# Splitting V into two fp16 halves: from ScalarE and VectorE to GpSimd, through an fp32 copy of Wh in SBUF

## What is computed

```
h  = max(layernorm(x), 0)
Wh = h @ W                                   # 8 x 2048 x 256
f1 = Wh @ a[:256];  f2 = Wh @ a[256:]
e  = leaky_relu(f1[:, :, None] + f2[:, None, :], 0.2)
attention = softmax(where(adj > 0, e, -9e15), axis=1)   # over rows i, for each column j
out = x + elu(attention @ Wh)
```

## Time and profile before

| | |
|---|---|
| median of 3 runs | 992.19 us (990.35 to 992.49) |
| the profiled execution's own time | 987.88 us |
| its span, first to last instruction | 986.1 us |
| mean granted TensorE clock | 0.987 of full speed |
| busy: TensorE (PE) | 950.0 us, 96% |
| busy: VectorE (DVE) | 920.7 us, 93% |
| busy: ScalarE (ACT) | 879.3 us, 89% |
| busy: GpSimd (POOL) | 645.3 us, 65% |

### The profile page before, as it was taken

How to read it: one execution, slowest core, us unless ns; L and a number is a source line. 1 busy time by engine, 2 the same in 40 slices (tenths; PEclk the granted TensorE clock), 3 DMA queues, 4 the chain that set the end, 5 groups by cost and what they waited for, 6 DMA issues and landing times.

```text
span 986.1 us, 23861 instructions
## 1 busy us (share of the span) xinstructions
PE 950.0 (96%) x8993; PEld 840.0 (85%) x8993; DVE 920.7 (93%) x1271; ACT 879.3 (89%) x1237; POOL 645.3 (65%) x676
## 2 busy tenths in 40 slices
PE   8878999999999999999999999999999999999996
PEld 6666888889888898888888888888988989898896
DVE  8799989999899998999989998999999999999975
ACT  4788989999999999999999899999999999898985
POOL 6567665776766776876767776677676775555540
PEclk8899999999999999999999999999999999999898
DMA  9477667889879889799979988979987978979724
GB/s 233 83 107 108 97 108 122 147 162 156 149 136 176 146 155 167 119 180 149 161 147 144 173 148 151 154 141 172 156 163 123 172 133 138 170 113 158 143 65 140
DMA packets 199093, 142.13 MB, mean 144 GB/s; under 512 B 7361, under 2 KB 187841, under 8 KB 198978
## 3 DMA queue, kind: packets, MB, share of 16 engines
q0 software_dynamic: 140160, 81.80, 61.5%
q1 hardware_dynamic: 58818, 58.81, 20.8%
HBM read 176.16 MB, written 16.84 MB: 196 GB/s over the span
## 4 chain that ended last, share of the span: by engine, by line
POOL 32%; PE 30%; issue 25%; DVE 5%; DMA 4%; ACT 2%; POOLq 0%; SPq 0%; DVEq 0%; ACTq 0%
POOL direct L896 10%; POOL xn L910 6%; POOL raw L882 5%; POOL inv L893 4%; PE acc L511 4%; PE acc L504 4%; PE acc L506 4%; PE tp L439 3%; PE acc_st L486 3%; PE acc_st L487 3%; PE acc_st L488 3%; POOL y L916 3%; PE pre L417 3%; POOL rstd L904 2%; POOL small_total L890 2%
## 5 line engine op out<-in xcount | busy, mean ns | idle before, releaser
L773 DVE CUSTOM_DVE_ANT_0 prob<-tp,f_row 128x2048 f32<-128x2048 bf16 x128 | 292.0, 2282 | 21.5 <-DMA f_row<-f_scratch 14.9
L590 ACT ACTIVATE prob<-prob,f 128x2049 f32<-128x2049 f32 x128 | 257.6, 2013 | 5.4 <-DVE prob L773 5.4
L486 PE MATMUL acc_st<-v,stored 128*128 128x256 f16 x960 | 261.5, 272 | 0.8 <-ACT part L620 0.8
L488 PE MATMUL acc_st<-v,stored 128*128 128x256 f16 x960 | 261.7, 273 | 0.0
L487 PE MATMUL acc_st<-v,stored 128*128 128x256 f16 x960 | 261.6, 273 | 0.0
L598 ACT ACTIVATE prob<-prob,shift 128x2048 f32<-128x2048 f32 x128 | 256.5, 2004 | 4.0
L896 POOL TENSOR_TENSOR direct<-prob,inv 128x1024 f16<-128x1024 f32 x128 | 243.5, 1902 | 10.0
L504 PE MATMUL acc<-v,direct 128*128 128x256 f16 x1024 | 233.4, 275 | 5.4 <-ACT z_direct L626 3.5
L506 PE MATMUL acc<-v,direct 128*128 128x256 f16 x1024 | 233.3, 274 | 0.0
L890 POOL TENSOR_SCALAR small_total<-total 128x1 f32<-128x1 f32 x128 | 29.8, 233 | 272.8 <-ACT prob L598 271.4
L604 ACT ACTIVATE stored<-prob,inv 128x1024 f16<-128x1024 f32 x128 | 146.1, 1142 | 47.6 <-POOL inv L893 47.6
(11 more groups left out here) (94 smaller groups left out, 1383.9 us busy)
## 6 DMA issues: line engine op xcount, KB each, us to landing
raw<-in_adj POOLq DMA_DIRECT2D x64, 1024.0 KB, 11.2
y<-in_x SPq DMA_DIRECT2D x63, 256.0 KB, 3.1
out<-y SPq DMA_DIRECT2D x63, 256.0 KB, 2.2
y<-elu POOLq DMA_DIRECT2D x56, 256.0 KB, 5.0
x_in<-in_x SPq DMA_DIRECT2D x108, 128.0 KB, 3.3
f_row<-f_scratch SPq DMA_DIRECT2D x31, 256.0 KB, 6.5
stored<-in_x SPq DMA_DIRECT2D x4, 512.0 KB, 6.9
f_scratch<-f_t SPq DMA_DIRECT2D x124, 0.5 KB
```

The lines of the kernel that those rows point to most:

```text
L486: nc.tensor.matmul(bank[:, 0:FO], p_st[:, 0, rows], v_c[:, 0, :], start=(c == 0), stop=False)
L488: last = nc.tensor.matmul(bank[:, 0:FO], p_st[:, 1, rows], v_c[:, 0, :], start=False, stop=(c == G - 1))
L590: nc.scalar.activation(p_top, p_top, ACT.Prelu, bias=f2, alpha=ALPHA).then_inc(leaky, 1)
L773: nc.vector.tensor_tensor_reduce(out=prob[:, c % 2, 0:N], in0=tp_b, in1=f1_row[:, b % 2, :], scale=1.0, scalar=-3.0e38, op0=ALU.add, op1=A ...
```

## The change

The high and the low half of V are both made on GpSimd by a new function `split_v`. GpSimd gets them from `wh_sb`, a single fp32 buffer in SBUF into which ScalarE now copies Wh (`keep_wh`) where it made the high half before. VectorE's `split_v_low` stays for the first 17 chunks only. The next transpose into the bank waits for ScalarE's copy (`wh_kept`) in place of `v_ready`. The copy of chunk c waits until GpSimd has made both halves of chunk c - 1 (`v_ready`), and `split_v` is put between `split_high` and `normalise` in GpSimd's step. Each chunk's direct matmuls wait for `v_ready` of their own chunk, which is 17 steps old. A few small columns are packed together, and the ring of f2 columns shrinks from 20 to 18, to make room for `wh_sb`.

```diff
-    RF = 20
+    RF = 18
+        wh_sb = sb("wh_sb", [P, FO], F32)
-        minus_half = sb("minus_half", [P, 4], F32)
...
+        cols = sb("cols", [P, 16], F32)
+        minus_half, minus_one, small_total = cols[:, 0:1], cols[:, 1:2], cols[:, 2:3]
+        shift, total, inv = cols[:, 4:6], cols[:, 8:12], cols[:, 12:16]
# TensorE, transpose_x(c), c > LEAD
-                    wait(pe, v_ready, c)
+                    if c == LEAD + 1:
+                        pe.wait_ge(v_ready, LEAD)
+                    pe.wait_ge(wh_kept, c - LEAD)
# TensorE, direct_blocks(c)
-                    pe.wait_ge(v_ready, LEAD)
+                pe.wait_ge(v_ready, max(c + 1, LEAD))
# ScalarE
+            def keep_wh(c):
+                act.wait_ge(v_ready, c)
+                nc.scalar.copy(wh_sb[:], wh_bank(c)[:, 0:FO]).then_inc(wh_kept, 1)
...
                 if chunk(s + LEAD):
                     take_f(s + LEAD)
-                    split_v_high(s + LEAD)
+                    keep_wh(s + LEAD)
# VectorE
-                if chunk(s + LEAD) and s != -1:
+                if s < -1 and chunk(s + LEAD):
                     split_v_low(s + LEAD)
# GpSimd
+            def split_v(c):
+                pool.wait_ge(wh_kept, c - LEAD + 1)
+                wait(pool, stored_done, c - RV - 7)
+                if c == LEAD:
+                    pool.wait_ge(v_ready, LEAD)
+                nc.gpsimd.tensor_copy(v[:, c % RV, 0, :], wh_sb[:]).then_inc(v_hi, 1)
+                pool.wait_ge(v_hi, c + 1)
+                nc.gpsimd.tensor_tensor(v[:, c % RV, 1, :], wh_sb[:], v[:, c % RV, 0, :], ALU.subtract
+                                        ).then_inc(v_ready, 1)
...
                 if chunk(s - 1):
                     split_high(s - 1)
+                if s >= 0 and chunk(s + LEAD):
+                    split_v(s + LEAD)
                 if chunk(s + LEAD + 2) and s >= 0:
                     normalise(s + LEAD + 2)
```

More of the change, by code:

```diff
@@ L146, in graph_attention @@
         v_ready = sem("v_ready")
+        wh_kept = sem("wh_kept")
         direct_done = sem("direct_done")
@@ L517, in extra_blocks @@
                 if c == LAST_BATCH:
-                    pe.wait_ge(v_ready, CH)
+                    pe.wait_ge(wh_kept, CH - LEAD)
                     pe.wait_ge(f_ready, CH)
@@ L579, in take_f @@
                 nc.scalar.copy(f12[:, i:j + 1:j - i], wh_bank(c)[:, FO:FW]).then_inc(f_ready, 1)
+            def keep_wh(c):
+                act.wait_ge(v_ready, c)
+                nc.scalar.copy(wh_sb[:], wh_bank(c)[:, 0:FO]).then_inc(wh_kept, 1)
             def split_v_high(c):
-                wait(act, stored_done, c - RV - 7)
                 nc.scalar.copy(v[:, c % RV, 0, :], wh_bank(c)[:, 0:FO]).then_inc(v_hi, 1)
@@ L591, in attention @@
                 act.wait_ge(leaky, c + 1)
-                nc.scalar.activation(shift[:, c % R:c % R + 1], prob[:, c % 2, N:N + 1], ACT.Copy, scale=-1.0
+                nc.scalar.activation(shift[:, c % 2:c % 2 + 1], prob[:, c % 2, N:N + 1], ACT.Copy, scale=-1.0
                                      ).then_inc(shift_s, 1)
@@ L597, in attention @@
                 wait(act, total_s, c - R + 1)
-                nc.scalar.activation(p, p, ACT.Exp, bias=shift[:, c % R:c % R + 1],
+                nc.scalar.activation(p, p, ACT.Exp, bias=shift[:, c % 2:c % 2 + 1],
                                      accum_out=total[:, c % R:c % R + 1]).then_inc(prob_ready, 1)
@@ L653, in _ @@
             act.wait_ge(const_ready, 1)
-            nc.scalar.activation(shift[:, R - 1:R], minus_one[:], ACT.Copy)
+            nc.scalar.activation(shift[:, 1:2], minus_one, ACT.Copy)
             scale_w()
@@ L866, in _ @@
             nc.gpsimd.memset(ident[:], 0.0).then_inc(memset_done, 1)
-            nc.gpsimd.memset(minus_half[:], -0.5)
-            nc.gpsimd.memset(minus_one[:], -1.0)
+            nc.gpsimd.memset(minus_half, -0.5)
+            nc.gpsimd.memset(minus_one, -1.0)
             nc.gpsimd.memset(ones, 1.0)
@@ L887, in split_high @@
                 k = inv[:, c % R:c % R + 1]
-                t = small_total[:, c % R:c % R + 1]
+                t = small_total
                 pool.wait_ge(prob_ready, c + 1)
@@ L892, in split_high @@
                 wait(pool, lo_stored, c - R + 1)
-                nc.gpsimd.tensor_tensor(k, t, minus_one[:], ALU.pow).then_inc(inv_ready, 1)
+                nc.gpsimd.tensor_tensor(k, t, minus_one, ALU.pow).then_inc(inv_ready, 1)
                 pool.wait_ge(inv_ready, c + 1)
@@ L903, in root @@
                 rs = slice(chunks.start % RS, chunks.start % RS + len(chunks))
-                nc.gpsimd.tensor_tensor(rstd[:, rs], var_eps[:, rs], minus_half[:, 0:len(chunks)], ALU.pow
+                nc.gpsimd.tensor_tensor(rstd[:, rs], var_eps[:, rs], minus_half.to_broadcast([P, len(chunks)]), ALU.pow
                                         ).then_inc(rstd_s, 1)
```

## The result

The changed kernel takes 1114.89 us (median of 4 runs, 1112.61 to 1116.38), the kernel before 992.34 (4 runs). The ratio is 1.1235, 95% interval 1.1208 to 1.1262: 12% slower, 122.6 us by the medians. The forecast was 1093 in a range of 1005 to 1145, and slower with 0.87.

What follows compares the result with a forecast made beforehand. TensorE was taken to bound the kernel at 7.26 us a step; GpSimd's round, grown to 8.19, would replace it: 103 us over 111 steps on 988, giving 1091, with half the median's offset 1093, range 1005 to 1145.

Steps and rivals of the forecast that it cites:

- TensorE's pace, and what VectorE's relief could buy: Steps 0 to 110: TensorE sets the pace at 7.26 us; relieving VectorE gives back at most 19.8 us.
- The cost of the two instructions: GpSimd behind direct: cast 0.40, subtraction 0.57, semaphore 0.08; these 1.05 us alone would fit into 2.1 us of room.
- Their place: Right after direct, VectorE's excluding instructions block GpSimd: cast, subtraction and xn end about 3.95 us after direct, before 0.95.
- mask-first order: If the mask comes first, cast waits for L762 (0.9), subtraction for L787 (to 2.4), xn for L792 (to 3.95).
- disturbed nobody: VectorE's 111 removed subtractions, 412 ns each, 45.7 us, with one input in PSUM, were said to disturb no other engine.
- The round: GpSimd's step: 3.95 + 1.04 + 0.35 + 2.85 = 8.19 us, above TensorE's 7.26, costing 103 us over 111 steps.
- Waits of ScalarE and TensorE's clock: ScalarE's copy and its new wait cost nothing, TensorE's transpose gets its bank earlier; nothing given for the clock.
- The early steps: Sign in the profile after: steps of 7.7 us at the start, without y DMAs, and 8.3 later.
- How long the port is held: Port free before the GpSimd instruction ends: L792 lost 0.15; by the skill's whole-instruction rule 0.35, time near 1103.
- A: Phases slip: direct ends some 0.9 us earlier against VectorE's step, GpSimd's round 7.24; about 1010 us, chance 0.2.
- B: The two GpSimd operations are dearer, 0.56 and 0.99: 64 us more, about 1157 us; chance 0.1.
- C: GpSimd's room holds the work, round under 7.26, VectorE's relief gains 3 to 15 us: about 983 us; chance 0.1.

Runs made afterwards that it cites:

- nolow: Kernel before without VectorE's split_v_low from chunk 17 on, matmuls reading the high half instead, output less exact: 988.96 us, ratio 0.9964.
- late: Changed kernel with split_v moved on GpSimd from behind split_high to the end of its step, behind normalise, DMA issues and root: 1035.8 us.
- readers: Kernel before plus a copy and a subtraction of 128x256 within wh_sb on GpSimd behind split_high, nobody waiting for them: 1109.73 us.
- writers: Kernel before plus three memsets of 128x256 fp32 on GpSimd behind split_high, which read nothing: 1072.39 us.
- cast: Changed kernel with only the high half made on GpSimd; VectorE still subtracts the low half from PSUM: 993.44 us, ratio 1.003.
- sub: Changed kernel with only the low half made on GpSimd; ScalarE casts the high half from PSUM and also copies Wh: 1063.56 us.
- after_gap: Changed kernel with VectorE's statistics moved from in front of the mask to behind it: 1084.82 us, ratio 1.0947.
- xn_first: Changed kernel with normalise put in front of split_v on GpSimd: 1121.89 us, ratio 1.1298.
- late_gap: Kernel late with VectorE's statistics moved from in front of the mask to behind it: 1029.92 us, ratio 1.0392.
- sub_gap: Kernel sub with VectorE's statistics moved behind the mask: 1019.82 us, ratio 1.0263, which leaves out one execution of 3423.87 us.

## Why the prediction was right, and where it was off

**TensorE's pace, and what VectorE's relief could buy.** Right. The prediction allowed a part of 19.8 us; nolow got about 3.

**The cost of the two instructions.** The cast alone was put at 0.40 and the shortest is 0.39; the subtraction at 0.57, and the shortest is 0.68, 0.11 more. As the prediction said, it isn't this that costs: 1.07 us alone would have fitted into 2.0 us of room.

**Their place.** This was the step that carried the forecast, and it held: cast, subtraction and `xn` were put at 3.95 us; they took 80.6, 165.8 and 184.4 us from step 0 to 110 of the changed kernel, together 430.8, 3.88 a step; from the end of `direct` to the end of `xn` it is 4.00 on average. The shift of single terms, 0.73, 1.49 and 1.66, is close to the mask-first order that the prediction gave as the second of its two. That the place is the cause is shown by late (the same instructions elsewhere, 79 us less) and readers (the same places without the change, 1109.73). What it left out is the window that `split_v_low` had been. The sum does have L787 right behind the mask, but the prediction said of the removed subtraction that it "disturbed nobody"; it even made room, as nolow shows: `xn` from 0.99 to 1.74.

**The round.** Forecast 8.19, measured 8.42, so 103 us against 128.4 of span; this term was undersized. The instructions of GpSimd in this stretch add up to 892.3 us, 14.0 of which overlap, and 56.3 are idle. Of these 32.3 are the short gaps between instructions, which the sum had in its start-to-start figures. The other 24.0 are waits: 10.8 for exp and 13.2 for `wh_sb`, 8.5 of these once, in step 0. That is 0.22 a step, which the sum had at nothing. The small terms nearly cancel: `root` 0.28 for 0.35, the DMA issues 1.04 as forecast, L894 and L897 0.32 and 0.63 on average where the timeline of a plain step has 0.24 and 0.58, for in some steps they too meet the mask L766 at the port. The waits are about as large as the miss; that the rest cancels is in part luck. The rounds are far from equal, too: without a DMA issue 7.30 us (15 rounds), with one 8.15 (69), with one and `root` 9.69 (20), with two and `root` 10.15 (6).

**Waits of ScalarE and TensorE's clock.** The new wait of `keep_wh` cost 2.5 us once (for VectorE's last low half in step 0), otherwise nothing of note. ScalarE's wait for `inv` grew by 137 us, 1.2 a step, a little more than the forecast 0.5 to 1; VectorE's for `direct`, 88.6, 0.8 a step, is in it. TensorE's idle time is not where the prediction looked: ahead of the matmuls of L505 (the old L504) it is 14.0 us, ahead of those of `make_wh` (L416) 59.4. Its transposes, which were to get the bank earlier at no cost, waited 33.8 us for the new copy, which stands behind the late `stored` in ScalarE's queue. GpSimd was busy for 94% of these steps, forecast 97%. The early steps, 2 to 13, took 7.8 us on average and those from 16 on 8.5, forecast 7.7 and 8.3. `xn`, at 1.70, is above the forecast means of 1.0 to 1.5, the subtraction, at 1.49, within. TensorE's busy share was put at 88% and is 88.2%. Its granted clock was 0.98 over these steps, for 1.00 before, and L505 takes 279 ns for 275; TensorE wasn't the bound, so it isn't in the sum.

**How long the port is held.** L796 was drawn out by 0.42 us by a subtraction that takes 0.68 alone (1.69 for 1.27). What is held against a two-input instruction is less than the whole. The Trainium skill ("SBUF — State Buffer", section "SBUF: two separate sides") has the pair of SBUF ports that VectorE and GpSimd share held for the whole instruction; the trace doesn't agree with the letter of it. The memsets of writers, which read nothing, ended while L790 ran, and took 0.42 us each on average, the mask's share in it. The Trainium skill ("SBUF — State Buffer", section "Who interferes with whom") says that a VectorE instruction with two SBUF inputs contends with a GpSimd instruction that reads SBUF and not with one that only writes; the trace agrees.

**The rivals.** A, phases that slip past each other at 7.24: no. The cast did run free of the mask in 37 of 111 steps (under 0.5 us), but the subtraction behind it met L791 in 104 of 111 all the same, and the round averaged 8.42. B, 0.99 and 0.56 alone: no. C: its condition, a round under 7.26, is met by cast (5.6 by the sum below) and nolow, not by the change.

**One rule for all runs.** Take from the changed kernel all but the pack and the waits: (934.6 - 430.8 - 24.0)/111 = 4.32 us. Add the last column of the table and compare with 7.26. late: 7.64, so 42 us over 992, measured 44. sub: 7.82, 62, measured 72. after_gap: 8.05, 88, measured 93. xn_first: 8.25, 110, measured 130. readers: 8.15, 99, measured 118. writers: 7.80, 60, measured 80. cast: 5.64 and nolow: 6.06, nothing, measured +1 and -3 (+3 and -3 against the before timed beside them). It gives the direction and most of the size; it is short by 2 to 20 us, and by 25 and 28 for late_gap (7.38) and sub_gap (7.05), where GpSimd's mean is about TensorE's and the 7 us of the moved statistics aren't in it. The rounds say more than the mean. In late_gap the 69 with one DMA issue take 7.52 us, 0.11 of it waiting for exp, those with `root` 8.10 (20) and, with two issues, 9.15 (6); the 15 without an issue take 6.99, of which 1.02 is waiting, so they give little back. In sub_gap the 69 take 7.51 too, but 0.42 of that is waiting: GpSimd's length isn't all of it there, and the rest is open.

**Who is passed over.** Where L787 or L792 (by whatever line number) has another two-input instruction right behind it, the timelines of all 13 kernels give a clean split. An `xn` issued between 0.06 us before the start of the first of the two and 0.04 us after it got in at its end, 138 times, as in step 1 of before. One issued 0.07 us into it or later always stood behind the next one too, 402 times, as the `xn` of writers that came 0.48 into L790. At 0.05 to 0.06 both happened. The cast, the copy and the subtractions were never passed over: 409 times they were issued more than 0.06 into such an instruction, and each got in at its end. So it is `xn` that is dear to push, and the price hangs on the instruction as well as on the place. `xn` alone of these takes two scalars from SBUF, a value for each partition; whether that is the reason no run tests.

## What to carry to other kernels

An engine's idle time is not its free capacity. Before work is moved to GpSimd, lay its timeline beside VectorE's and see what VectorE does at that moment: next to instructions with two SBUF inputs or the mask, 1.07 us of work became 2.2, and another 0.7 fell on the instruction behind it. An instruction that is taken away may have been the window that a neighbour used; ask of each removal who ran beside it. Here the split is best left where it was: none of the versions that compute the whole result is faster than the kernel before, and the one that comes next (cast, 0.3% slower) gains nothing by it.

## What the runs showed of the hardware that I had not expected

- Three memsets on GpSimd end beside a VectorE instruction with two SBUF inputs, but they move the reader behind them: `xn` 2.22 us for 0.99.
- `xn` can be kept out by two of VectorE's in a row, if it is issued as little as 0.07 us into the first: it took 2.44 us on average in sub, 0.55 alone. The cast and the subtraction never were.
- A short VectorE instruction that reads one operand from PSUM (0.41 us) is enough of a window for an `xn` of 0.55: 0.67 on average in cast, where a semaphore holds the subtraction to that place, 0.99 in before, and 1.74 in nolow without it.
